# Folding a unit's 36 weighted samples per channel to nine before the reduction

## What is computed

```
samp = _grid_sample(img, sg)       # 9 points per pixel and group, 4 corners each
mr = mask.reshape(n, H * W, G, P).transpose(0, 2, 1, 3).reshape(n * G, 1, H * W, P)
dout = (samp * mr).sum(-1)         # over the 9 points
```

## Time and profile before

| | us |
|---|---|
| median of 3 runs | 6882.04 (6880.75 to 6884.6) |
| the profiled execution | 6879.93 |
| its span in the trace | 6878.1 |
| busy: GpSimd | 4449.0 (65%) |
| busy: VectorE | 5163.5 (75%) |
| busy: TensorE | 3711.9 (54%) |
| busy: ScalarE | 1123.8 (16%) |

### The profile page before, as it was taken

One profiled execution on the slowest core, in us unless ns is written; L12 is line 12 of the kernel. 1 busy time (PEld: TensorE's weight loads), 2 busy tenths in 40 slices (PEclk: granted clock), 3 DMA queues, 4 the chain that ended last, 5 costly groups with the idle time before them and its releaser, 6 DMA issues.

```text
span 6878.1 us, 44571 instructions
## 1 busy us (share of the span) xinstructions
PE 3711.9 (54%) x11426; PEld 1961.4 (29%) x11426; DVE 5163.5 (75%) x4236; ACT 1123.8 (16%) x1698; POOL 4449.0 (65%) x4683
## 2 busy tenths in 40 slices
PE   7145251351575525653765336635747664297879
PEld 4022131220232213421322114312323442143544
DVE  5879788887787768976777669876877897635455
ACT  2010100101111002221110012211110222111345
POOL 1777677777777777777777777777777777700000
PEclk9577675675787767876887668767878887698989
DMA  4463553644444333465443334564443346510148
GB/s 133 137 178 106 181 144 121 207 130 159 145 132 132 105 108 122 132 206 198 131 132 117 108 110 132 169 217 142 132 132 105 122 132 208 172 37 25 64 154 231
DMA packets 529644, 954.06 MB, mean 139 GB/s; under 512 B 268544, under 2 KB 325632, under 8 KB 513408
## 3 DMA queue, kind: packets, MB, share of 16 engines
q0 software_dynamic: 221184, 604.27, 28.3%
q1 hardware_dynamic: 308352, 348.52, 15.5%
HBM read 792.21 MB, written 160.24 MB: 138 GB/s over the span
## 4 chain that ended last, share of the span: by engine, by line
POOL 44%; issue 20%; DVE 13%; PE 12%; DMA 3%; ACT 1%; SPq 1%; POOLq 0%; DVEq 0%; ACTq 0%
POOL ring L441 44%; PE PS L820 11%; DVE ring L1580 4%; DVE dbuf L1586 2%; DMA ring<-table,idx_stage 1%; ACT img L1241 1%; DVE sm L2044 1%; DMA img<-d_dram 1%; DVE sm L2067 1%; DVE sm L2060 1%; DVE img L2013 0%; DVE img L2071 0%; DVE stats L1642 0%; DVE wb_sb L2078 0%; SPq L705 0%
## 5 line engine op out<-in xcount | busy, mean ns | idle before, releaser
L441 POOL DMA_INDIRECT ring<-table,idx_stage x4608 | 4431.7, 962 | 1432.1 <-issue 1368.2
L1586 DVE TENSOR_REDUCE dbuf<-ring 128x64 f32<-128x2304 f32 x512 | 2073.2, 4049 | 28.5
L820 PE MATMUL PS<-img,wb_sb 128*128 128x512 f32 (+1 forms) x3264 | 1615.7, 655 | 502.8 <-DVE img L1900 264.0
L1580 DVE TENSOR_TENSOR ring<-ring,PS 128x2304 f32<-128x2304 f32 x480 | 1224.4, 2551 | 606.7 <-DMA ring<-table,idx_stage 595.7
L820 PE MATMUL PS<-img,wa_sb 128*128 (+2 forms) x2848 | 841.1, 632 | 598.1 <-DVE img L1996 226.5
L820 PEld LDWEIGHTS PS<-img,wb_sb 128*128 128x128 f32 x3264 | 676.9, 212 | 1407.4 <-issue 960.1
L820 PEld LDWEIGHTS PS<-img,wa_sb 128*128 128x128 f32 (+1 forms) x2848 | 368.8, 164 | 1041.0 <-issue 979.0
L489 POOL MEMSET img<- 128x192 f32 x1 | 0.3, 258 | 672.9 <-DMA o_dram<-img 672.9
L1241 ACT ACTIVATE img<-PS,sm 128x512 f32<-128x512 f32 x384 | 247.5, 680 | 1027.1 <-PE PS L820 1022.8
L820 PE MATMUL PS<-wa_sb,cb 128*128 128x108 f32 (+1 forms) x1024 | 238.4, 399 | 322.5 <-DVE cb L1647 257.4
L820 PE MATMUL PS<-sm,params 128*128 128x4 f32 x28 | 7.7, 350 | 703.3 <-DVE sm L1626 691.9
(11 more groups left out here) (235 smaller groups left out, 3247.4 us busy)
## 6 DMA issues: line engine op xcount, KB each, us to landing
ring<-table,idx_stage POOLq DMA_INDIRECT x4608
table<-cb SPq DMA_DIRECT2D x64, 512.0 KB, 6.3
img<-y_dram SPq DMA_DIRECT2D x64, 512.0 KB, 6.6
q_dram<-img SPq DMA_DIRECT2D x32, 1024.0 KB, 4.3
img<-q_dram SPq DMA_DIRECT2D x28, 1024.0 KB, 7.1
img<-in_x SPq DMA_DIRECT2D x8, 2048.0 KB, 11.6
y_dram<-cb SPq DMA_DIRECT2D x64, 256.0 KB, 2.2
img<-in_x SPq DMA_DIRECT2D x32, 512.0 KB, 5.9
```

The costliest lines, as they stand in the source:

```text
L441: nc.gpsimd.indirect_dma_start(out=ring[:, g, p * CORNERS * GC:(p + 1) * CORNERS * GC], out_offset=None, in_=tab[b], in_offset=bass.Indire ...
L820: return nc.tensor.matmul(o, l, r, start=start, stop=stop, **kw)
L1580: last = vec.tensor_tensor(rg, rg, weights.unsqueeze(2).to_broadcast([P, n, GC]), ALU.mult)
L1586: vec.tensor_reduce(dbuf[:, j, g * GC:(g + 1) * GC], ring[:, g, :].rearrange("p (k c) -> p c k", c=GC), AX_X, ALU.add).then_inc(sem("ring_ ...
```

## The change

The 2304 products of a unit lie in four quarters of 576 (9 x 64) values. Two additions put quarter 2 onto quarter 0 and quarter 3 onto quarter 1, a third puts quarter 1 onto quarter 0, all in place in `ring`, and the reduction then reads quarter 0 alone, nine values per channel. `weighted` goes up three times in a unit, and VectorE waits for it three times: ahead of the first pair, ahead of the third addition, and ahead of the reduction.

```diff
                 last.then_inc(sem("weighted"), 1)
-                dve.wait_ge(sem("weighted"), t * G + (b * TILES * G + g + 1))
+                steps = t * (3 * G) + (b * TILES * 3 * G + 3 * g)
+                dve.wait_ge(sem("weighted"), steps + 1)
+                size = K2 * CORNERS * GC // 4
+                quarter = [ring[:, g, q * size:(q + 1) * size] for q in range(4)]
+                vec.tensor_tensor(quarter[0], quarter[0], quarter[2], ALU.add)
+                vec.tensor_tensor(quarter[1], quarter[1], quarter[3], ALU.add).then_inc(sem("weighted"), 1)
+                dve.wait_ge(sem("weighted"), steps + 2)
+                vec.tensor_tensor(quarter[0], quarter[0], quarter[1], ALU.add).then_inc(sem("weighted"), 1)
+                dve.wait_ge(sem("weighted"), steps + 3)
                 if g == 0:
 
                     dve.wait_ge(sem("d_stored"), t * 16 + (16 * b * TILES + 16 - 16 * j))
-                vec.tensor_reduce(dbuf[:, j, g * GC:(g + 1) * GC], ring[:, g, :].rearrange("p (k c) -> p c k", c=GC),
+                vec.tensor_reduce(dbuf[:, j, g * GC:(g + 1) * GC], quarter[0].rearrange("p (k c) -> p c k", c=GC),
                                   AX_X, ALU.add).then_inc(sem("ring_free"), 1)
```

## The result

The changed kernel takes 7075.15 us (median of 4 runs, 7067.85 to 7076.88) where the kernel before takes 6881.4 beside it: 1.028 times as long, 95% interval 1.0262 to 1.0293. 194 us slower; 195 were forecast. The profiled execution is the lowest of its four, 7067.85 us with a span of 7066.1, 188 us longer than that of before.

What follows compares the result with a forecast made beforehand. GpSimd's unbroken gathers were taken to bound the stream: holds of 68 + 132 = 200 us, less 5 for slots, added to 6882 give 7077 us. Own range 7005 to 7128; 8 times in 10, 6985 to 7155.

Steps and rivals of the forecast that it cites:

- nothing to hide it: GpSimd in the stream: it works without a pause, so 195 us more moves its last gather from 6014 to about 6209.
- The hold: GpSimd's gathers: a request falling into a VectorE instruction with two SBUF inputs waits for its end, 0.33 to 0.43 us a unit.
- 200 less 5: GpSimd's list: 200 us of holds by the additions, less 5 us gained at slot waits, 195 us in all.
- Units tied to a landing: 205 units that start when their ninth gather lands, so at a fixed phase to GpSimd: 0.33 us each, 68 us.
- The others: 307 units whose requests come at an evenly spread moment against the additions: 0.43 us each, 132 us.
- the 51 us: GpSimd's waits for slots in the stream, 53 in number: the upper bound of the gain, of which 5 us were taken.
- The free first moments: VectorE's additions: a request within 0.14 us of an addition's start passes unheld; without this, 0.54 us a unit as upper bound.
- Held more: Rival: additions hold requests from their first moment and units lose their tie, 0.54 us in all 512; 7153 us, chance 0.15.
- held less: Rival: units settle where a request comes late in the second addition, 0.18 us each; 6949 us, chance 0.13.
- Faster: Rival: additions inside one buffer do not hold GpSimd, half of the slot waits are gained; 6857 us, chance 0.03.
- no change: Rival: reduction time saved, nothing held and no slot wait shortened, or both small and equal; 6880 us, chance 0.03.
- cover: VectorE's 317 us saved over 512 units only lengthen its waits for gathers, worth only what GpSimd waited for slots.

Runs made afterwards that it cites:

- e4: Kernel before with its reduction reading only the first nine values of each channel, no additions; 6864.25 us, ratio 0.9963 to the kernel before.
- e1: Changed kernel with the three additions replaced by one-input reductions of the same size, in place; 6885.87 us, ratio 0.9995 to the kernel before.
- e2: Changed kernel with the additions' second input in PSUM in 480 of 512 units; 6892.37 us, ratio 1.0003 to the kernel before.
- e6: Changed kernel with one addition of 128x1152 for the three, 18 values per channel reduced; 7113.26 us, ratio 1.032 to the kernel before.
- e5: Changed kernel without the third addition, 18 values per channel reduced; 7040.41 us, ratio 1.0211 to the kernel before.
- e7: Changed kernel with each addition cut into three pieces of 128x192; 6931.19 us, ratio 1.0058 to the kernel before.
- e3: Changed kernel with its additions kept and the reduction reading all 36 values again; 7415.56 us, ratio 1.0764 to the kernel before.
- e9: Changed kernel with each addition cut into nine pieces of 128x64; 7522.82 us, ratio 1.0918 to the kernel before.
- e8: Kernel before, without the fold, with four of its own two-SBUF-input instructions cut into shorter ones; 6857.72 us, ratio 0.9964 to the kernel before.
- e10: Changed kernel with each addition cut into four pieces of 128x144; 6920.43 us, ratio 1.0053 to the kernel before.
- e12: As e11, with one more VectorE wait on itself between the first six and second six pieces; 6933.95 us, ratio 1.0072 to the kernel before.
- e11: Changed kernel with each addition cut into six pieces of 128x96; 7112.06 us, ratio 1.033 to the kernel before.

## Why the prediction was right

**The bound.** The stream is GpSimd's. e4 shows it from one side (1481 us taken from VectorE, 26 gained), the last gather's place from the other (187 of 188 us of the longer span lie ahead of it). The step "nothing to hide it" held.

**The reduction.** 1134 ns forecast, 1129 measured; additions 759 and 753 to 759; VectorE 4790 us busy forecast, 4797 measured. Between 576 and 2304 elements the step of 64 values costs (4049 - 1129)/1728 = 1.69 ns an element, the figure of the prediction.

**The hold.** The mechanism was argued from the earlier trace rows and is shown by e1 and e2: with one SBUF input or the second in PSUM the loss is gone. That it lasts to the instruction's end is shown by e6 against e5, by e7, and by the changed kernel's own records: nine in ten of its 639 gathers held by an addition end between 0.815 and 0.822 us behind that addition's end. Counted over the changed kernel's records (a request is 0.126 us behind a gather's start, its hold is what the gather takes over 0.946): 371 requests fell in the second addition and cost 109 us, 188 in the first, 40 us, 150 in the third, 33 us. Together 181 us.

**The sum.** It was 200 less 5. Two terms were off, and they made up for one another. Units tied to a landing: 205 x 0.33 forecast; there are some 293 now, since VectorE waits more often, at 0.34 each, 101 us instead of 68. The others: 307 x 0.43 forecast; 219 at 0.37, 80 us instead of 132. That their phases are not even may be why; it was not shown. So 181 and not 200. Three terms the sum had too small or not at all. 14 us were won at slots, not 5 (the 51 us that the prediction had as their bound contain 53 ordinary gaps, so no more than 34 could be won). 196 - 181 = 15 us of hold were added outside the new additions, most of it in the leaky ReLU, whose holds rose from 20 to 29 us. And the copies of line 457 cost 5 us more. In net 181 - 14 + 15 + 5 = 187, all of the last gather's delay. The median's 194 is 6 more than the profiled execution's 188, as that one was the quickest of four. The agreement within a microsecond is luck, and even that within ten rests on terms that were off by up to 52 us and made up for one another. What was earned is the mechanism, the engine that bounds the stream and a price of about a third of a microsecond a unit.

**The free first moments.** The prediction took 0.14 us in which an addition holds nothing, from a single row. In the changed kernel all 42 requests that came 0.06 to 0.14 us behind the start of an addition passed, and none of those that came 0.18 us or more behind it.

**The rivals.** "Held more" needed 0.54 a unit, "held less" 0.18; 0.35 was measured (181/512). "Faster" and "no change" needed additions that don't hold; e1 and e2 show what the time is then. The rule of the Trainium skill, SBUF — State Buffer, section "Who interferes with whom", that two SBUF inputs contend with a GpSimd instruction that reads SBUF, fits the holds, and e1 and e2; its inference that a `tensor_tensor` leaves descriptor generation alone does not fit these gathers, whose indices are read from SBUF (1.30 us against 0.95 in the rows above). That the index read is what is held was not tried by itself. The copies of line 457 make no descriptors, read and write SBUF, and are held too. In the kernel before none of the 60 takes over 0.27 us; in the changed kernel 13 take 0.37 to 0.78, and each ends 0.10 us behind the end of an addition of the fold (seven) or of line 2079, which has two SBUF inputs as well (six).

**What was wrong** beyond these terms lay not in the prediction but in expectations behind it: in e3 "cover" was taken for the whole stream where one stage had 7 us of 316 and others fell short too; in e9 a rule seen on pieces of 0.75 us was carried to trains of 18 pieces of 0.22.

## What to carry to other kernels

Ask first which engine's list the time is made of, and what a shorter list on another engine would buy: here 1481 us of VectorE bought 26. Where GpSimd makes descriptors without a pause, as here, each VectorE instruction with two SBUF inputs is a possible hold of up to its own length; put the second input in PSUM (e2), use one input (e1), or cut it into pieces of 144 to 288 columns (e7, e8, e10), and don't let more than six or seven of them follow one another without a wait (e12). Spare time is counted stage by stage, not over the span.

## What the runs showed of the hardware

- In these records a gather has one moment at which it is held, 0.126 us behind its start; after the hold it takes 0.82 us whatever it waited. A two-input instruction does not hold it in its first 0.14 us or so: in the changed kernel 42 of 42 requests that came 0.06 to 0.14 us behind the start of an addition passed, and in e7 550 of 1006 requests that fell within an addition of 0.36 us did.
- Trains of short instructions join. With 128x144 (next start 0.219 us behind the last), 128x96 (0.169 us) and 128x64 (0.135 us) alike, requests get in between until the eighth piece of a train has started; after that nearly all wait for the end of the train, up to 2522 - 946 = 1576 ns in e9. A wait of VectorE on itself, some 0.035 us of idle time, lets requests in and starts the count anew (e11 against e12: 178 us). The number of pieces decides here and not the time, since the eighth starts 0.95 us into the train in e9 and 1.53 us in e10. Why it is that number no run shows.
